# Mamba-2 block and mixture of experts on one core: the expert loop, the shared layer and the last norms as two pipelined loops in one block

## What is computed

```
x = x + layernorm(mamba2(layernorm(x)))
t = layernorm(x)                                   # 8192 tokens of 256
gu = t @ shared_gate_up_w                          # 256 -> 2 x 512
shared = (silu(gu[:, :512]) * gu[:, 512:]) @ shared_down_w * sigmoid(t @ shared_gate_w)
w, idx = top_k(softmax(t @ gate_w), 8);  w = w / w.sum()
buf[e, slot] = t[token]                            # first 128 tokens of each expert, by a running count
act = silu(buf @ Wg[e]) * (buf @ Wu[e])            # 256 -> 2 x 128
y[token] += w * (act @ Wd[e])                      # dropped where the count is over 128
x = x + layernorm(y + shared)
```

## Time and profile before

| | before |
|---|---|
| median of 3 runs | 1656.42 us (1653.9 to 1657.65) |
| profiled execution, its own time | 1650.5 us |
| its span, first to last instruction | 1648.8 us |
| PE, DVE, ACT, POOL busy | 81%, 71%, 57%, 52% |
| mean granted TensorE clock | 0.928 |

### The profile page before, as it was taken

How to read it: one execution, slowest core, us unless ns; L and a number is a source line. 1 busy time by engine, 2 the same in 40 slices (tenths; PEclk the granted TensorE clock), 3 DMA queues, 4 the chain that set the end, 5 groups by cost and what they waited for, 6 DMA issues and landing times. The chain is left out here.

```text
span 1648.8 us, 29343 instructions
## 1 busy us (share of the span) xinstructions
PE 1342.8 (81%) x8642; PEld 1132.7 (69%) x8642; DVE 1169.3 (71%) x3361; ACT 946.9 (57%) x2128; POOL 865.5 (52%) x1103
## 2 busy tenths in 40 slices
PE   3889999999999999999999983788888888888300
PEld 2677777877777778778777763677777777787300
DVE  4788888888988988889888874344544445445297
ACT  3667678677676776776767766233433334333143
POOL 0454654645546545455565461455545555555298
PEclk9999999999999999999999996799999999999755
DMA  5301000001000000000000003445444444454365
GB/s 187 117 8 35 28 27 29 27 29 33 27 29 27 27 29 27 29 33 27 29 27 21 17 28 107 123 109 125 110 105 111 116 116 110 109 122 111 77 198 159
DMA packets 110616, 115.51 MB, mean 70 GB/s; under 512 B 19632, under 2 KB 98800, under 8 KB 110576
## 3 DMA queue, kind: packets, MB, share of 16 engines
q1 hardware_dynamic: 95440, 90.38, 17.3%
q0 software_dynamic: 14336, 23.08, 8.1%
q10 hardware_dynamic: 800, 1.57, 0.3%
HBM read 68.53 MB, written 46.47 MB: 70 GB/s over the span
## 5 line engine op out<-in xcount | busy, mean ns | idle before, releaser
L1010 POOL TENSOR_TENSOR mamba_arena<-mamba_arena 128x512 f32<-128x512 f32 (+1 forms) x352 | 383.4, 1107 | 193.5 <-DVE mamba_arena L782 144.9
L782 DVE TENSOR_TENSOR mamba_arena<-bank,mamba_arena 128x512 f32<-128x512 f32 (+1 forms) x192 | 114.9, 599 | 88.0 <-ACT mamba_arena L757 52.6
L1385 PE MATMUL bank<-xt_hi,wsgu_hi 128*128 128x256 f32 x512 | 148.3, 290 | 4.7 <-DVE xt_lo L1317 4.7
L1327 DVE TENSOR_SCALAR_CACHE_REDUCE experts_arena<-experts_arena 128x128 f32<-128x128 f32 x64 | 22.2, 347 | 183.2 <-DMA experts_arena<-count_table,row_now 183.2
L1385 PE MATMUL bank<-xt_lo,wsgu_hi 128*128 128x256 f32 x512 | 145.7, 285 | 0.0
L1385 PE MATMUL bank<-xt_hi,wsgu_lo 128*128 128x256 f32 x512 | 145.7, 284 | 0.0
L452 PE MATMUL bank<-identity,mamba_arena 128*128 128x128 f32 x704 | 103.2, 281 | 31.8 <-ACT mamba_arena L652 31.2
L1519 ACT ACTIVATE experts_arena<-bank_s,experts_arena 128x256 f32<-128x256 f32 x64 | 26.8, 471 | 177.9 <-DMA routed_sum<-experts_arena,scatter_now 177.9
L1261 POOL DMA_INDIRECT routed_sum<-experts_arena,scatter_now x64 | 104.1, 1627 | 47.3 <-issue 32.1
L452 PEld LDWEIGHTS bank<-identity,mamba_arena 128*128 128x128 f32 x704 | 83.2, 146 | 58.0 <-ACT mamba_arena L652 35.6
L1429 PE MATMUL bank_s<-wsdown_hi,act_hi 128*128 128x256 f32 x256 | 87.6, 342 | 38.9 <-DVE act_lo L1310 38.9
(11 more groups left out here) (270 smaller groups left out, 4664.2 us busy)
## 6 DMA issues: line engine op xcount, KB each, us to landing
experts_arena<-in_egu SPq DMA_DIRECT2D x64, 256.0 KB
routed_sum<-zeros SPq DMA_DIRECT2D x1, 8320.0 KB, 27.0
x_all<-in_x SPq DMA_DIRECT2D x32, 256.0 KB, 2.6
token_table<-mamba_arena SPq DMA_DIRECT2D x64, 128.0 KB, 1.7
normed_transposed<-mamba_arena SPq DMA_DIRECT2D x32, 256.0 KB, 2.0
experts_arena<-normed_transposed SPq DMA_DIRECT2D x32, 256.0 KB
experts_arena<-in_edown SPq DMA_DIRECT2D x64, 128.0 KB
experts_arena<-routed_sum SPq DMA_DIRECT2D x32, 256.0 KB, 3.0
```

Source lines behind the costliest of these rows:

```text
L782: return nc.vector.tensor_tensor(out, a, b, op)
L1010: return nc.gpsimd.tensor_tensor(out, a, b, op)
L1327: nc.vector.tensor_scalar(below, slot_counts[:, m, :], slot, None, ALU.is_le, ALU.add, accum_out=offset[:, m:m + 1]).then_inc(offset_ready, 1)
L1385: last = nc.tensor.matmul(half_up[c][:, f * 256:(f + 1) * 256], w[:, k, columns], x[:, k, :], start=n == 0, stop=n == len(parts) - 1)
```

## The change

The expert stage and the norm stage become one block with two loops. `pairs` and `rounds` go; each engine has a written-out order of operations per step, `iteration_r1` and `iteration_r2`, in which the operations of a step belong to up to three successive items (`j0 = i`, `j1 = i - 1`, `j2 = i - 2`).

- First loop, 16 steps: four experts (two pairs, `u` = 0 and 1, each with its own `rows`, `wgu`, `wdown`, `act_e`, `out_e`, indices) and one shared tile (tiles 0 to 15).
- Second loop, 8 steps: two shared tiles (16 to 31), and four groups of the norm: two for tiles whose shared result the first loop kept in `shared` (groups `2*j0` and `2*j0 + 1`), and two for tiles that this loop computed, where VectorE takes the down products straight from PSUM, multiplies by the gate and adds the routed sum in one operation.
- The activation uses the Silu function of ScalarE and one product on VectorE, in both layers; the factors of the gate and the weights change accordingly.
- The copies of row and token indices move from GpSimd to VectorE; `gather_now` is written by VectorE directly.
- PSUM: the chunks of the shared tile go to banks that other products use in the same step.
- In the Mamba stage some twenty semaphore increments for which nobody waits are dropped, and the last, empty iteration.

```diff
-                        last.then_inc(b_turned, 1)
+                        last
...
-        def pairs(eng, iteration, first, last):
...
-            lo, hi = 2, PAIRS - 2
...
+        def pipeline(eng, iteration, first, last, end):
+            for i in range(first):
+                iteration(i)
+            if last > first:
+                with eng.Fori(first, last) as i:
+                    iteration(i)
+            for i in range(last, end):
+                iteration(i)
@@ GpSimd, first loop @@
+                def iteration_r1(i):
+                    j0, j1, j2 = i, i - 1, i - 2
+                    if real(j2, 16):
+                        eng.wait_ge(added01, 16 * j2 + 16)
+                        eng.wait_ge(out_e_ready1, j2 + 1)
...
+                    if real(j2, 16):
+                        eng.wait_ge(added10, 16 * j2 + 16)
...
+                    if real(j1, 16):
+                        if real(j1 - 1, 16):
+                            eng.wait_ge(added11, 16 * j1)
+                        eng.wait_ge(out_e_ready0, j1 + 1)
+                        eng.wait_ge(scatter_kept0, j1 + 1)
...
+                pipeline(eng, iteration_r1, 4, 16, 18)
@@ ScalarE, first loop @@
+                        if real(j1 - 1, 16):
+                            eng.wait_ge(added01, 16 * j1)
+                        eng.wait_ge(down_e_done0, j1 + 1)
+                        eng.wait_ge(weight_kept0, j1 + 1)
+                        for m in range(2):
+                            last = nc.scalar.activation(out_e[:, 0, m, :], bank[4][:, m * DM:(m + 1) * DM], ACT.Copy, scale=slot_weight[:, 0, m:m + 1])
...
-                    nc.scalar.activation(tanh_s[:, c], half_up[c][:, 0:256], ACT.Tanh, scale=0.5).then_inc(tanh_s_ready[c], 1)
+                        nc.scalar.activation(silu_s[:, 0, 1], bank[2][:, 0:NB * P], ACT.Silu).then_inc(silu_ready1, 1)
-                    nc.vector.scalar_tensor_tensor(act_s[:, c], tanh_s[:, c], 1.0, half_up[c][:, 0:256],
-                                                   ALU.add, ALU.mult).then_inc(act_s_half[c], 1)
-                    nc.vector.tensor_tensor(act_s[:, c], act_s[:, c], half_up[c][:, 256:512],
+                        nc.vector.tensor_tensor(act_s[:, 0, 1], bank[2][:, NB * P:2 * NB * P], silu_s[:, 0, 1], ALU.mult).then_inc(act_ready1, 1)
@@ SyncE, second loop @@
+                def iteration_r2(i):
+                    j0, j1, j2 = i, i - 1, i - 2
+                    if real(j0, 8):
+                        if is_number(j0) and j0 == 0:
+                            eng.wait_ge(added11, 256)
+                        eng.nop(nofuse=True)
+                        eng.dma_start(routed[:, 1], tokens_of(routed_d[0:TOK, :], 2 * j0 + 0)).then_inc(routed_loaded1, 16)
+                    if real(j0, 8):
+                        eng.nop(nofuse=True)
+                        eng.dma_start(xt[:, 0].rearrange("p k t -> p (k t)"), xnt_d[bass.ds(2 * j0 + 16, 1), :, :].rearrange("o p f -> (o p) f")).then_inc(xt_loaded, 16)
@@ VectorE, second loop: gated shared tile from PSUM plus routed sum @@
+                            last = nc.vector.scalar_tensor_tensor(f_sum[:, 0, b, :], bank[1][:, b * DM:(b + 1) * DM], gate_s[:, 0, b:b + 1],
+                                                                  routed[:, 0, b, :], ALU.mult, ALU.add)
+                pipeline(eng, iteration_r2, 4, 8, 10)
```

More of the change, by code:

```diff
@@ L403, in pipeline @@
                 iteration(i)
-            for i in range(STEPS - AHEAD, STEPS + DEPTH_1 + 1):
+            for i in range(STEPS - AHEAD, STEPS + DEPTH_1):
                 iteration(i)
@@ L752, in iteration @@
                     if real(j0):
-                        nc.scalar.activation(xbc[:, 0:KI], half[:, 0:KI], ACT.Silu).then_inc(xc_ready, 1)
+                        nc.scalar.activation(xbc[:, 0:KI], half[:, 0:KI], ACT.Silu)
                     if real(j1):
@@ L1143, in build @@
-        down_s_done, gate_s_ready, shared_ready = sem("down_s_done"), sem("gate_s_ready"), sem("shared_ready")
-        counts_v = counts_d.rearrange("(i e) t -> e i t", e=NE)
-        half_up = [bank[k][:, :] for k in range(4)]
-        down_s = bank_s[:, 0, :]
-        down_e = bank_s[:, 1, :]
-        up_e = bank[4][:, :]
-        turn_e = bank[5][:, :]
-        def pairs(eng, iteration, first, last):
-            lo, hi = 2, PAIRS - 2
-            for q in range(first, lo):
-                iteration(q, None)
-            with eng.Fori(lo, hi) as q:
-                iteration(q, True)
-            for q in range(hi, last):
-                iteration(q, None)
@@ L1540, in build @@
-        f_const, f_power, f_scale, f_applied, f_ready = sem("f_const"), sem("f_power"), sem("f_scale"), sem("f_applied"), sem("f_ready")
-        def rounds(eng, stages):
-            def one(i):
-                for u in range(DEPTH):
-                    for stage, behind in stages:
-                        if not (is_number(i) and i * DEPTH + u < behind):
-                            stage(i * DEPTH + (u - behind), i + (u - behind) // DEPTH, (u - behind) % DEPTH)
-            one(0)
-            with eng.Fori(1, ROUNDS - 1) as i:
-                one(i)
-            one(ROUNDS - 1)
-            for g in range(GROUPS, GROUPS + max(behind for _, behind in stages)):
-                for stage, behind in stages:
-                    if g - behind < GROUPS:
-                        stage(g - behind, (g - behind) // DEPTH, (g - behind) % DEPTH)
@@ L1644, in _ @@
-                rounds(eng, [(power, 0), (add_residual, 1)])
+                nc.gpsimd.iota(past_end, pattern=[[1, P]], base=1, channel_multiplier=0,
+                               allow_small_or_imprecise_dtypes=True).then_inc(iotas, 1)
+                nc.gpsimd.iota(slot, pattern=[[1, 1]], base=0, channel_multiplier=1,
+                               allow_small_or_imprecise_dtypes=True).then_inc(iotas, 1)
+                nc.gpsimd.iota(expert, pattern=[[1, NE]], base=0, channel_multiplier=0,
+                               allow_small_or_imprecise_dtypes=True).then_inc(iotas, 1)
```

1227 lines of the change are left out of this document (794 added, 433 removed).

## The result

The changed kernel takes 1561.97 us in the median of four executions, the kernel before 1655.16 us on the same chip. Three of the four lie at 1559.65 to 1563.95 us; the fourth took 1698.22 us at a granted clock of 0.73 against their 0.93, counts in the median and not in the ratio. The ratio is 0.943, with an interval of 0.941 to 0.946: faster, by 93 us. I had predicted 1530 us with a range of 1505 to 1595. The direction and the range hold; the forecast is 30 to 32 us short, at the upper edge of its own range of 1512 to 1560.

What follows compares the result with a forecast made beforehand. The prediction took a ring of waits on scatters, not TensorE, to bound the expert loop. Its stage terms ended the span at 1522.8 us, 126 less than 1648.8; 1656.4 - 126.0 gave 1530 us, range 1505 to 1595.

Steps and rivals of the forecast that it cites:

- What bounds now: Old kernel: expert loop bound by a ring of waits, then norms alone; about 92 us gained by norms going beneath matmuls.
- Start, 1066 us: From tables in place at 1036.2 us to GpSimd's third first-loop step, the first with all four scatters, at 1066 us.
- First loop, 19.0 us a step: First loop: four chained scatters at 4.66 us make 18.6 us, with loop registers 19.0 us a step, for fourteen steps.
- rival 2: First loop: DMA queues fill and each of 61 chained scatters lands 1 us later; 1591 us, chance 0.15.
- Rival 1: Both loops: loads cover the scatter chain, GpSimd's issue and TensorE's 17.5 us set the steps; about 1508 us, chance 0.10.
- Last scatters and hole, 32.3 us: Between the loops: five scatters and the last landing, 27.4 us, then TensorE waiting 4.9 us for token tiles.
- Second loop, 18.6 us a step: Second loop: TensorE's 17.5 us plus one blockage of VectorE by GpSimd, 1.03 us; bounds 17.5 and 20.9 us.
- The lock-out that I charged at 1.03 us: Second loop: a short VectorE operation delayed during a GpSimd addition; about one such blockage shows a step, 1.03 us.
- the slow start after the pause: Second loop's first tile: TensorE at 1.2 GHz at first, its 48 up matmuls taking 7.7 us instead of 5.83, 1.9 us.
- Drain, 8.9 us: After the last matmul: gated sum, statistics, norm passes, last addition and 3.0 us to the end of the span, 8.9 us.
- The median: Whole kernel: the old median, 1656.4 us, lies 5.9 us above its profiled execution; the 126.0 us gain was subtracted from it.
- rivals 2 and 3: Rival 3, in the second loop: VectorE and GpSimd bound the step at 20.9 us; 1549 us, chance 0.14.

Runs made afterwards that it cites:

- old-stage kernel: Changed kernel with the Mamba stage written as before, its unawaited increments and empty last turn back: 1562.33 us in the median, ratio 0.943.
- two sums: Changed kernel, second expert of each pair adding into a second, unread table, each scatter waiting for the last but one: first-loop step 20.46 us.
- early tiles: Changed kernel with the second loop's first token tiles loaded before SyncE's wait for the scatters, that step's norms last on VectorE and ScalarE: 1556.03 us, ratio 0.940.
- narrow additions: Changed kernel with the second loop's four residual additions a step cut to one column: second-loop step 17.28 us against 17.53.
- weights once: Changed kernel with the eight expert weight loads of a first-loop step run only for the first step: step 18.89 us, execution 1543.11 us.

## Why the prediction was right, and where it was short

*What bounds now.* Right: the norms' 92 us without a matmul went beneath the second loop, and that is most of the gain. The other parts of the change (Silu for tanh, the copies moved to VectorE) were not run by themselves, so what they are worth is not shown.

*Start, 1066 us.* Forecast 8.1 us too early. Of these, 4.45 us are the Mamba stage, which I said "stays": its code does, its duration does not, as the old-stage kernel and the five rows above show. The profile of before that I took it from has the earliest end of all fourteen profiles. The remaining 3.7 us are mine. The tables were waited for till 1040.41; from there I allowed 12.5 us to the first expert matmuls, which took 14.7 (1055.07), because the first count gather began 1.06 us behind the tables and four in a row delay the first landing; GpSimd's next gathers then waited 2.6 and 2.8 us for row numbers that VectorE writes behind other waits.

*First loop, 19.0 us a step.* This is the term that failed: 20.90. The mechanism was right, since the four scatters are the chain and neither GpSimd's issue nor TensorE ends a step; the price of a link was not. I took 4.66 us from the end of the old loop, where nothing ran beside it, for a loop whose transfers I had myself put at 3.2 MB a step. That traffic (3.26 MB measured) lengthens a link to 5.22 us on average: rival 2, at half the 1 us that I gave it. It is beyond both marks that I had set myself, a step of at most 20.5 us and a link of at most 5.2. With the weights gone the link is 4.72 us and the step 18.89, 0.1 us from my figure. GpSimd's issue, 17.7 in the forecast, should read 17.6 from its own terms and measures 18.0 with two sums. Rival 1 is out: the rows show GpSimd waiting 3.06 us behind 1.56 us of issue even in the quiet tail. By the Trainium skill, "DMA: Bandwidth & Descriptors", "Anatomy of one DMA — SWDGE (gpsimd) path", 128 KB should have landed in an estimated 2.3 us; the trace disagrees with that estimate.

*Last scatters and hole, 32.3 us.* Right: 31.6. Five links of 4.5 to 4.7 us, a landing and the loads; TensorE is idle for the last 20.50 us of it. The kernel with early tiles shows that the 20 us were a place in SyncE's queue.

*Second loop, 18.6 us a step.* 17.53: nearer the lower bound, TensorE's 17.5. The lock-out that I charged at 1.03 us costs at most 0.25. The Trainium skill's rule ("SBUF — State Buffer", "SBUF: two separate sides"), by which the step would have tended to 20.9, describes what VectorE suffers. The trace agrees with it as far as VectorE goes, 2.1 us a step by the narrow additions and a subtraction of 1.22 us in place of 0.41; the step did not tend to 20.9, since VectorE has time to spare beside TensorE's 17.28 us. The first two steps took 19.3 and 18.5 us, 2.7 more than two steady ones. With narrow additions the first two are 1.5 more, so the slow start after the pause is within my 1.9 us, and the rest goes with the additions.

*Drain, 8.9 us.* 16.6. I listed the operations and left out two transfers' places. The last routed tile is loaded only at 1543.22, behind SyncE's waits for two norms, and VectorE waits 5.25 us for it; loading it earlier took 4.4 us off. And from the last addition's end (1552.1) to the end of the span it is 6.1 us, where the earlier trace rows gave 3.0.

*The median.* I added 5.9 us, the distance of before's median from its profile. The changed kernel's median lies only 2.0 us above its profile, and its executions at 1559.65 and 1563.95 us 0.3 below and 4.0 above it. That fits what was said of the start: before's profiled execution has an early end of the Mamba stage.

*What the range owes to luck.* The forecast's own terms miss the span by 35.4 us, 26.6 of them in one; the stated range holds the result because I had stretched it to 1595 for rivals 2 and 3, not because the sum was good to that.

## What to carry to other kernels

A landing time read at the quiet end of a loop is a lower bound for the busy middle: before using it for a chain, work out the bytes that will move beside it and price the link from a stretch with that traffic, here some 1.3 us a step for each MB at first and 1.9 later. A step of the program that is moved ahead of a wait pays only if everything queued behind it on each in-order engine is re-sorted too: of a 20.5 us hole, 18 closed in one edit and 11 came back elsewhere. And before comparing two spans, compare the ends of a stage whose code is the same.

## What the runs showed that I had not expected

- The Mamba stage, with identical code, ended between 1022.6 and 1037.7 us over the runs (by the start of the sum over the count table), in the main later where TensorE's mean granted clock was lower (1024.07 us at 0.964 in the changed kernel, 1037.68 at 0.950 with weights once).
- With a second table as target of the scatters, TensorE's semaphore for one group of matmuls came 1 to 5 us behind the end that their rows show, in step after step, at a granted clock of 1.00; what slows TensorE there is open. A late reader whose row says "remote" can be one that was told late.
- With TensorE at 100.00 us busy in 100, a step was still 0.25 us longer than its matmuls take without a gap.
- One more megabyte a step, loaded into a buffer that nobody reads, made each step 1.9 us longer, though no engine that computes waits for those loads.
